# Who issues the loads of a front stage: GpSimd takes half of W and of the first x, and W comes in pieces of 256 rows

## The reference

```python
Bx   = einsum('bni,bri->bnr', x, cond_B[ids])        # rank 16
cond = einsum('bnr,bor->bno', Bx, cond_A[ids])       # back to 2048
base = einsum('bsi,oi->bso', cond, W) + bias         # W: 2048 x 2048
res  = einsum('bsi,ri->bsr', cond, ffn_A)            # rank 64
prob = softmax(einsum('bsi,ei->bse', cond, router))  # 16 experts
comb = weights of the two best experts, normalized
delta = einsum('bse,bsr,eor->bso', comb, res, ffn_B) # ffn_B: 16 x 2048 x 64
out  = x + base + 0.5 * delta
```

## Time and profile before

| | us |
|---|---|
| median of 3 runs (lowest, highest) | 481.87 (481.14, 483.77) |
| the profiled execution: its own time | 482.06 |
| the profiled execution: span from first to last instruction | 480.2 |
| busy TensorE, VectorE, ScalarE, GpSimd | 420.9, 287.2, 108.9, 47.9 |
| mean granted TensorE clock | 0.968 |
| bytes moved | 135.29 MB, mean 282 GB/s |

### The profile page before, as it was taken

How to read it: one execution, slowest core, us unless ns; L and a number is a source line. 1 busy time by engine, 2 the same in 40 slices (tenths; PEclk the granted TensorE clock), 3 DMA queues, 4 the chain that set the end, 5 groups by cost and what they waited for, 6 DMA issues and landing times.

```text
span 480.2 us, 5829 instructions
## 1 busy us (share of the span) xinstructions
PE 420.9 (88%) x2112; PEld 255.5 (53%) x2112; DVE 287.2 (60%) x635; ACT 108.9 (23%) x166; POOL 47.9 (10%) x54
## 2 busy tenths in 40 slices
PE   0296286988988999999999999999999999999996
PEld 0143065533535665556656655675565567557575
DVE  1472412488755657776675777667677756777353
ACT  0010013332654423012202201330230023013200
POOL 4601000000120002001200200120021012001100
PEclk9998766899999999999999999999999999999999
DMA  9999999994999779889999988998898899744854
GB/s 211 223 286 318 292 314 311 268 294 130 355 252 335 228 243 367 276 289 335 317 292 287 377 288 278 329 323 289 286 376 309 272 308 343 270 166 158 284 215 176
DMA packets 105811, 135.29 MB, mean 282 GB/s; under 512 B 13812, under 2 KB 67060, under 8 KB 105780
## 3 DMA queue, kind: packets, MB, share of 16 engines
q1 hardware_dynamic: 68708, 99.45, 63.3%
q10 hardware_dynamic: 37074, 35.46, 26.6%
HBM read 99.24 MB, written 35.65 MB: 281 GB/s over the span
## 4 chain that ended last, share of the span: by engine, by line
PE 69%; DVE 12%; ACTq 10%; issue 3%; DMA 2%; ACT 2%; DVEq 0%
PE ps L842 12%; PE ps L859 12%; PE ps L860 10%; PE ps L861 10%; PE ps L807 7%; PE ps L872 7%; DVE xT L677 5%; PE ps L862 5%; ACTq L277 4%; PE ps L797 4%; DVE h_r L659 3%; ACTq L293 3%; ACTq L241 2%; DVE xbuf L785 2%; DMA early_u<-in_L_ffn_B 2%
## 5 line engine op out<-in xcount | busy, mean ns | idle before, releaser
L785 DVE TENSOR_TENSOR xbuf<-ps,xbuf 128x512 f32<-128x512 f32 x128 | 87.0, 679 | 106.2 <-PE ps L862 106.0
L859 PE MATMUL ps<-h_r,u_r 128*128 128x512 f32 x256 | 109.2, 427 | 7.0 <-DVE xbuf L785 7.0
L807 PE MATMUL ps<-early 128*128 128x512 f32 x128 | 69.1, 672 | 36.5 <-DVE early L597 21.3
L860 PE MATMUL ps<-h_r,u_r 128*128 128x512 f32 x256 | 100.3, 392 | 0.0
L861 PE MATMUL ps<-h_r,u_r 128*128 128x512 f32 x256 | 100.2, 391 | 0.0
L859 PEld LDWEIGHTS ps<-h_r,u_r 128*128 128x128 f32 x256 | 48.0, 188 | 47.9 <-issue 20.1
L677 DVE STREAM_TRANSPOSE xT<-xbuf 128x512 f32<-128x512 f32 x112 | 72.1, 682 | 0.0
L842 PE MATMUL ps<-bexpT,cur 128*32 128x512 f32 x512 | 61.6, 598 | 2.1 <-DVE h_r L659 2.1
L807 PEld LDWEIGHTS ps<-early 128*128 128x128 f32 x128 | 24.5, 211 | 66.0 <-issue 39.5
L619 DVE STREAM_TRANSPOSE early<-xbuf 128x512 f32<-128x512 f32 x64 | 41.9, 686 | 24.7 <-DMA xbuf<-in_L_ffn_base_w 12.7
L452 ACT ACTIVATE h_r<-ps 128x512 fp32r<-128x512 f32 x64 | 35.7, 594 | 86.2 <-issue 53.9
(11 more groups left out here) (64 smaller groups left out, 222.7 us busy)
## 6 DMA issues: line engine op xcount, KB each, us to landing
out<-xbuf SPq DMA_DIRECT2D x31, 1024.0 KB, 7.0
xbuf<-in_x SPq DMA_DIRECT2D x30, 1024.0 KB, 7.0
xbuf<-in_x SPq DMA_DIRECT2D x28, 512.0 KB, 8.3
xbuf<-in_x ACTq DMA_DIRECT2D x28, 512.0 KB, 9.4
xbuf<-in_L_ffn_base_w SPq DMA_DIRECT2D x16, 512.0 KB, 18.5
xbuf<-in_L_ffn_base_w ACTq DMA_DIRECT2D x16, 512.0 KB, 18.8
early_u<-in_L_ffn_B ACTq DMA_DIRECT2D x12, 512.0 KB, 9.5
gm_r<-g_hilo SPq DMA_DIRECT2D x128, 32.0 KB, 6.1
```

Of the source, the lines that this page charges most:

```text
L785: dve.tensor_tensor(xs, ps[:, ACC + t % 2, :], xs, ALU.add).then_inc(s_out, 1)
L807: pe.matmul(ps[:, ACC + g % 2, :], a_t[:, s, :], wT[:, n % RING, :], start=(s == 0), stop=(s == KD - 1)).then_inc(s_wmm, 1)
L859: pe.matmul(acc, u_r[:, b.q, 0, h, tok_t], hi, start=(h == 0), stop=False)
L860: pe.matmul(acc, u_r[:, b.q, 0, h, tok_t], lo, start=False, stop=False)
```

## The change

W now comes in 8 pieces of 256 rows by all columns, still 2.1 MB each, with runs of 512 floats (2 KB). A slice is 128 x 256, so there are 128 of them (`NW`), the ring `wT` has 8 places, and all tables of positions are written anew in the new unit. Quarters 2 and 3 of W and of the first sample are issued by GpSimd; SP keeps quarters 0 and 1 and loses `cond_B`, the small matrices and the experts, all of which go to ACT. The experts' flips 0 to 7 stand earlier among W's products, and groups 14 and 15 use other buffers.

```diff
-RING = 4
+RING = 8
...
-    NW = W_GROUPS * KD
+    PIECES = 2 * W_GROUPS
+    NW = PIECES * KD
...
-    w_q = base_w.rearrange("(g t l) (q d) -> g q l t d", t=BANK // SQ, l=SQ, q=NQ)
+    w_q = base_w.rearrange("(g t l) (q d) -> g q l t d", t=WN // SQ, l=SQ, q=NQ)
...
-        X_AT = {38 + i: (2 * i, 2 * i + 1) for i in range(8)}
-        BX_AFTER = {42: 4, 46: 8}
-        SLOT_AT = {47: 8, 49: 9, 52: 10, 54: 11, 56: 12, 59: 13, 61: 14}
+        X_AT = {80 + 2 * i: (2 * i, 2 * i + 1) for i in range(8)}
+        BX_AFTER = {88: 4, 96: 8}
+        SLOT_AT = {98: 8, 102: 9, 107: 10, 110: 11, 113: 12, 118: 13, 122: 14}
...
-        E_AT = {18: 0, 21: 1, 24: 2, 27: 3, 31: 4, 35: 5, 39: 6, 43: 7, 48: 8, 52: 9, 55: 10, 59: 11}
-        E_LATE = {0: 12, 1: 13, 3: 14, 5: 15}
-        E_SLOT = (0, 1, 2, 0, 1, 2, 0, 1, 2, 0, 1, 3, 0, 1, 0, 1)
+        E_AT = {12: 0, 20: 1, 30: 2, 38: 3, 50: 4, 58: 5, 66: 6, 74: 7, 97: 8, 104: 9, 111: 10, 119: 11}
+        E_LATE = {0: 12, 1: 13, 2: 14, 5: 15}
+        E_SLOT = (0, 1, 2, 0, 1, 2, 0, 1, 2, 0, 1, 3, 0, 1, 3, 0)
...
-            need(eng, s_wt, (n - WB + 1) * KH)
+            need(eng, s_wt, (n - WB + 1) * KD)
             for q in qs:
-                eng.dma_start(w_in[n % WB][q * SQ:(q + 1) * SQ], w_q[n // 2, q, :, :, n % 2 * XD:(n % 2 + 1) * XD])\
-                   .then_inc(s_load[n % WB], 16)
+                eng.dma_start(w_in[n % WB][q * SQ:(q + 1) * SQ], w_q[n, q]).then_inc(s_load[q // 2][n % WB], 16)
...
-                pe.matmul(ps[:, ACC + g % 2, :], a_t[:, s, :], wT[:, n % RING, :], start=(s == 0),
-                          stop=(s == KD - 1)).then_inc(s_wmm, 1)
+                pe.matmul(ps[:, ACC + g // 2 % 2, g % 2 * WN:(g % 2 + 1) * WN], a_t[:, s, :], wT[:, n % RING, :],
+                          start=(s == 0), stop=(s == KD - 1)).then_inc(s_wmm, 1)
```

More of the change, by code:

```diff
@@ L99, in adaln_ffn @@
         bexpT = sb("bexpT", [P, OC, NP, BANK])
-        with (nc.sbuf_tensor("early", [P, 2, KD // RING, BANK], F32) as early,
+        with (nc.sbuf_tensor("early", [P, 2, RING, WN], F32) as early,
               nc.sbuf_tensor("early_u", [P, 2, 2, EG, ET * R], F32) as early_u):
@@ L159, in adaln_ffn @@
         s_tok, s_conda, s_condb, s_small, s_bias = sem("tok"), sem("conda"), sem("condb"), sem("small"), sem("bias")
-        s_load = [sem(f"w_loaded{k}") for k in range(WB)]
+        s_load = [[sem(f"w_loaded{k}_half{h}") for k in range(WB)] for h in range(2)]
         s_ein = [sem(f"expert_in{k}") for k in range(4)]
@@ L164, in adaln_ffn @@
         s_xres = [sem(f"xres{c}") for c in range(NC)]
-        s_x0 = sem("x0_loaded")
+        s_x0 = [sem(f"x0_loaded_half{h}") for h in range(2)]
         s_xquad = [sem(f"xquad{g}") for g in range(2)]
@@ L321, in _ @@
             load_cond_a(sp, range(0, NAD // 2))
[L322 to L331, removed]
+            for n in range(1, 6):
+                load_w(sp, n, (0, 1))
             load_x0(sp, (0, 1))
-            load_w(sp, 5, (0, 1))
             store_g(0)
@@ L405, in _ @@
             ids = [adapter(pool, b) for b in range(NB)]
+            load_w(pool, 2, (2, 3))
+            load_w(pool, 3, (2, 3))
             pool.wait_ge(s_bias, 32)
@@ L420, in _ @@
                     .then_inc(s_bsel, 1)
+            load_w(pool, 5, (2, 3))
+            load_x0(pool, (2, 3))
+            for n in range(6, PIECES):
+                load_w(pool, n, (2, 3))
             def front(f):
@@ L454, in _ @@
             act.dma_start(tok[:, :], itok.rearrange("(a b) -> a b", a=1)).then_inc(s_tok, 16)
-            load_w(act, 0, (2, 3))
             load_cond_a(act, range(NAD // 2, NAD))
-            load_w(act, 1, (2, 3))
-            load_cond_b(act, (2, 3))
+            load_cond_b(act, range(NQ))
             act.wait_ge(s_const, 1)
-            load_small(act, (2, 3))
-            load_w(act, 2, (2, 3))
-            load_w(act, 3, (2, 3))
+            load_experts(act, 0)
+            load_small(act, range(NQ))
+            for g in range(1, E_FIRST):
+                load_experts(act, g)
             act.wait_ge(s_idn, 2)
@@ L549, in _ @@
                     load_xquad(act, 1, 1, (2, 3))
-                if n >= GHI_AT and n % KD == GHI_AT % KD:
-                    g_hi(n // KD - 1)
+                if n >= GHI_AT and n % (2 * KD) == GHI_AT % (2 * KD):
+                    g_hi(n // (2 * KD) - 1)
                 if n in E_AT:
@@ L611, in w_transpose @@
                 g, s = n // KD, n % KD
-                piece = n // KH
-                if n % KH == 0:
-                    dve.wait_ge(s_load[piece % WB], (piece // WB + 1) * NQ * 16)
+                if s == 0:
+                    for half in range(2):
+                        dve.wait_ge(s_load[half][g % WB], (g // WB + 1) * NQ // 2 * 16)
                 need(dve, s_wmm, n - RING + 1)
@@ L666, in x_transpose @@
                     if j == 0:
-                        dve.wait_ge(s_x0, NQ * 16)
+                        for half in range(2):
+                            dve.wait_ge(s_x0[half], NQ // 2 * 16)
                 else:
@@ L674, in x_transpose @@
                 if f.n == 1 and j == XRING // 2:
-                    dve.wait_ge(s_ef, E_FRESH + 1)
+                    dve.wait_ge(s_ef, max(g for g in range(GROUPS) if E_SLOT[g] == E_SLOT[E_FRESH]) + 1)
                 need(dve, s_bxq, f.n * KD + j - XRING + 1)
```

49 lines of the change are left out of this document (23 added, 26 removed).

## The result

The changed kernel takes **494.71 us** (median of 4 runs, 493.31 to 496.37); the kernel before, measured again beside it, 481.5. The ratio is **1.0272**, 95% interval 1.0219 to 1.0326: 13 us slower, where 475 us was forecast. The profiled execution took 494.57 us, its span 492.4 (before 480.2).

A forecast was written before the change was run, and what follows sets the result against it. It took bytes and issue order on full DMA engines to bind up to 98.7 us, engine work after. From 482.06 us, -5 - 1.5 - 0.7 gave 474.9, forecast as 475 us, range 466 to 488.

The forecast's parts named there:

- Part 1: Start: `cond_A` lands later beside GpSimd's W packets, so TensorE starts 4 to 10 us later; no term of its own.
- Part 2: Up to the sample's first slice: bytes come faster with 2-KB runs on both queues; -5 us, bounds -14 and +9.
- hinge: The sample's first transpose, at 98.7 us before; bytes and issue order decide ahead of it, engine work behind; forecast 92 to 101.
- ACT's chain: Ahead of the hinge: expert loads in turn on ACT's ring, 7 us each, ending at 92 to 101 us.
- Part 3: From the hinge to the tile stage: less work left in the tail, against a cost of shorter slices; -1.5 us.
- The two flips: Flips 7 and 6, moved ahead of the hinge; with two W products they take 3.5 us off the tail.
- Part 4: Tile stage: group 14, loaded early into the fourth buffer, no longer waits for its DMA; -0.7 us.
- "issue" waits: Ahead of the hinge: ACT's copies late because ACT stands issuing DMAs; forecast gone or under 10 us.
- A: Ahead of the hinge: the DMA rate does not change, more queues add no engine; 480 us, chance 0.2.
- B: Start: `cond_A` starves and the chain of expert loads shifts with it; 484 to 490 us, chance 0.17.
- C: Ahead of the hinge: GpSimd issues slowly, up to 5.9 us per DMA; 490 to 500 us, chance 0.08.
- D: Ahead of the hinge: full rate of 401 GB/s, hinge at 86 us; 466 to 470 us, chance 0.1.

The follow-up runs named there:

- e1_gate: The changed kernel, but GpSimd issues W pieces 1 to 3 only when all of `cond_A` has landed; 491.2 us, ratio 1.0202.
- the square: Four kernels with 2-KB pieces, places of before or of the change: SP and ACT issuing 1.0028 and 1.0173, GpSimd issuing its half 1.0128 and 1.0272.
- e2_shape: The changed kernel with issuers as before (GpSimd issues nothing), keeping its 2-KB pieces, ring, flip places and buffers; 488.38 us, ratio 1.0173.
- e11_early: e5_places with only expert flips 0 to 7 moved to the changed kernel's places; 490.46 us, ratio 1.0139.
- e7_same: The kernel before with SP issuing quarters 0 and 2, ACT 1 and 3, of W and the first sample; 497.57 us, ratio 1.0361.
- e4_share: e1_gate with `cond_B`, the small matrices and expert groups 0 to 2 split between SP and ACT as before; 496.41 us, ratio 1.0335.
- e8_halves: The kernel before with loads of expert groups 0 to 9 split by partitions, 0 to 63 on SP, 64 to 127 on ACT; 483.5 us, ratio 1.0033.
- e10_step: e5_places with expert groups 0 to 9 split by partitions over SP and ACT, and G's first store behind W piece 6; 481.46 us, ratio 0.9999.
- e5_places: e2_shape with all tables at twice the numbers of the kernel before, leaving only the 2-KB pieces of the change; 480.92 us, ratio 1.0028.
- e3_issuer: The kernel before (1-KB runs, old tables) with GpSimd issuing quarters 2 and 3 of W and the first sample; 502.47 us, ratio 1.0475.

## Why the prediction was wrong

**Part 1, start 4 to 10 us later, absorbed.** Mostly absorbed it was (e1_gate: 14 us earlier `cond_A`, 3.5 us earlier end), but it was 15.9. Three steps of the sum failed. "SP's piece 0 (512 packets) goes in step with GpSimd's first 512": GpSimd issued at 1.33 us, but its first packets moved at about 6.5, when SP's piece 0 was nearly through, so the two came one after the other. Its queue began some 5 us after an issue later too (last section); why, no run here shows. "4 x 2 x 256 = 2048 packets of 2 KB", each at 5.0 to 9.1 ns: they were 1024 of 4096 bytes and 128 small ones, and a round took 17.8 ns (281 in 5 us). That makes 20.5 us of rounds, near the upper end of the 15.5 to 21.5 us that the sum had for them, but they carried only 1152 of SP's `cond_A` packets, 56 per us where they do 610 alone. And the last of SP's, from 31 to 33 us, went packet for packet beside ACT's `cond_B` (283 and 289 in 2 us), which the sum had moving alone.

**Part 2, hinge -5 us.** It came +10.1. Two sentences of it failed. "W and sample are now 2 KB on both queues, so the halves stay in step": with a third queue of 4-KB packets beside SP's of 2 KB they don't (1.66 and 0.90 MB in the same ten us), and the rate fell to 278 instead of rising to 338 (issuer: 4.8 us by the square). And ACT's chain: one 1-KB and two 2-KB packets a round was the model, 7 us for a load; with 1 + 2 + 4 KB and 456 of ACT's packets in 10 us, a group's 512 take 11.2 us, and each waits besides for what stands ahead of it in the ring (16.5 us median to landing, up to 29.9). I had this chain's end at 92 to 101 and let it bound the forecast from below, but priced the earlier flips as a pure gain of the tail. The mean rate is only a part of it: e2_shape has before's 299 GB/s, both queues and a `cond_A` at 21 us, and still loses 1.73%. **The term missing from the sum was the cost of the new places**, put at nothing ahead of the hinge: 7 us, larger than any term in it, and 5 of them from the flips alone (e11_early). It could be had from rows: the prediction put group 0 near 39 us and each next one 7 us later, while flips 0 and 1 stood 12 and 20 slices (5.2 and 8.7 us of work) behind a first product that it put at 25 to 31 us. The prediction's reading of the earlier trace rows as one half alone was wrong as well (see e7_same), though the 225 GB/s it took from there was near what one half does.

**Part 3, -1.5 us.** +1.6. The two flips did leave the tail, yet the tail grew. A slice of 256 columns takes VectorE 0.34 us (3.38 for ten), not 0.32, so 0.03 a slice is right, though 0.32 less half of 0.61 is 0.015: the 1.4 us in the prediction came out right by a slip, and so by luck. I took a third of it as exposed; were it all, that would be 1 us. The first tile's h products took 3.24 us at a granted clock of 0.62 (154 to 157.6 us), where they took 1.92 before: 1.3 us, and no step had it. Of the 3.1 us by which I was off these explain up to 2.3; the rest isn't settled.

**Part 4, -0.7 us.** +0.45. The wait for an expert's DMA is gone as said; the waits of these flips for ScalarE's copies went from 1.2 to 2.0 us.

**Said and seen.** The "issue" waits ahead of ACT's copies (38.3 us before) are gone, as forecast, and gave nothing: the copies then waited for TensorE's flips, 49.8 us up to 154 us. Only ACT's first instruction still stands behind its issues, to 37.4 us (31.3 before).

```profile
ACT bexpT L449 <- PE ps L790: 49.8, 8, 18.1
```

**The rivals.** *A* (the rate does not change) was right that nothing was to be had from a third queue; the rate fell. The rule of the Trainium skill that it cites (DMA: Bandwidth & Descriptors, Rules for kernel authors), that spreading DMAs saves only issue time, is too mild for this case: by the square the issuers' change cost 1.0%, and GpSimd's half alone on 1-KB runs 4.75%. *B* had the sign and one of its two conditions was met (`cond_A` after 27 us; group 0's flip came at 44.73, just short of 45), but its cause, the shift of the chain by `cond_A`, is worth 3.5 of 13 us; its 484 to 490 was short by the places. *C* named the right engine for a wrong reason: an issue takes 0.6 us (1.30 for two), not 5. Its time, 490 to 500, was hit by luck. *D* was far off.

**What stays open.** Of the issuer's 4.8 us, how much is small packets starved and how much is halves out of step: both come from the 4-KB turn, and no kernel here had one without the other (e7_same shows only what the halves can cost by themselves). How much of it is the move of `cond_B`, the small matrices and the first experts to ACT, with GpSimd on 2-KB runs. Why e4_share lost 1.3% to e1_gate. And whether the edit of e8_halves raises the rate on 1-KB runs as it does on 2-KB ones (36 GB/s, e10_step against e5_places); its time doesn't tell, and its one profile, at 299 GB/s, is of an execution 2.6 us over the median.

## What to carry to other kernels

Before a load moves to another queue, ask how many bytes that queue moves in one turn and how many the others do: turns were equal here and bytes were not, and the transfers with the smallest packets paid. Give each half of the partitions the same bytes per turn, and split what belongs to neither (here the experts) in two. And an operation moved ahead in an in-order engine's list needs its data's new arrival beside its new due time: some 5 of 13 us here were one line of such a table. Then see that what is won isn't handed back by an engine that issues in front of the last copy.

## What the runs showed of the hardware

- GpSimd's queue moved 4096-byte packets from runs of 2 KB and of 1 KB alike (in the changed kernel and in e3_issuer 10.49 MB in 2848 packets, of which 288 are the small ends). SP's and ACT's moved one run a packet (834 of 2 KB against 833 of 1 KB). The Trainium skill (DMA: Bandwidth & Descriptors, Queues, rings and completion order) says that an engine takes turns between its queues by packets, each of some 9 to 17 descriptors; the turns are here, but on SP's and ACT's queues a turn was a single run: in half a microsecond on 16 engines, from 66.0 us of the kernel before, the two moved 52 and 50 packets, in the next half 50 and 50, which is some three per engine.
- 128-byte packets moved at 56 per us and queue beside GpSimd's 4096-byte ones (281 in 5 us), and 587 of them in the microsecond in which these ran out.
- GpSimd's queue moved its first packets 4 to 6 us after an issue that found it empty: none before 6 us for the issue at 1.33 us, none before 49.5 for the one at 43.95, none before 69 for the one at 64.70, and in e1_gate none before 25.5 for the one at 20.93. SP's, issued to at 0.74 us in the kernel before, had moved 18 packets by 2 us.
- At a DMA share of 0.99 to 1.10 the mean rate from 42 to 98.7 us lay between 239 and 334 GB/s over the kernels. Two pairs differ in one thing each, or nearly so: 300 and 240 by which half each queue fed (the kernel before and e7_same), 298 and 334 by the experts' loads split by halves over both queues (e5_places and e10_step). The share of busy time says nothing about it.
- Two queues that both fed the same half at a time made 240 GB/s, two that fed one half each 300 (e7_same against the kernel before).
